# Half of the 64x64 products of a block inverse sent crosswise between the row halves of TensorE

## The chip, the cores and the metric

One core of one Trainium2 chip runs the whole program. The metric is the time of one execution on the device in microseconds (us), the median of the runs shown. Engines are TensorE (PE, its weight loads PEld), VectorE (DVE), ScalarE (ACT), GpSimd (POOL) and SyncE (SP, which here only issues DMAs).

## What is computed

The reference adds three things to x (8 batches, 512 tokens, 256 features): a gated delta rule attention over 32 value heads, a small feed-forward part, and x itself. What this change touches is inside the attention, which works on chunks of 64 tokens. For each chunk it needs the inverse of a unit lower triangular 64x64 matrix, and the reference builds it row by row:

```
attn = -(jnp.einsum('bhcid,bhcjd->bhcij', k_beta, k) * decay_mask)
attn = jnp.where(upper, 0.0, attn)
def _correct_row(a, i):
    row = a[..., i, :]
    corr = jnp.einsum('...j,...jk->...k', row, a)
    corr = corr * (jnp.arange(chunk_size) < i)
    return (a.at[..., i, :].set(row + corr), None)
attn, _ = jax.lax.scan(_correct_row, attn, jnp.arange(1, chunk_size))
attn = attn + jnp.eye(chunk_size, dtype=attn.dtype)
value_corrected = jnp.einsum('bhcij,bhcjd->bhcid', attn, v_beta)
```

After that a state is carried from chunk to chunk (eight chunks), and each chunk's output is normed, gated and projected.

## The kernel before

The eight batches go in four pairs, and for each pair there are 16 key heads with two value heads each: 64 turns of one loop body, called heads here. A pair's two batches lie on the two halves of the 128 partitions: batch 0 on partitions 0 to 63, batch 1 on 64 to 127. A head has 16 units (8 chunks times 2 value heads), each a 64x64 matrix per batch; unit `u` of batch `b` is `tile[half(b), u, :]`.

No scheduler decides the order. Each engine has its own instruction stream, written by the same skeleton: `core` walks the eight chunks of head g, and between its steps it calls `front_piece` for head g + 1, with a step number s from 0 to 23 (three per chunk). So a piece with s = 19 or 20 lies in chunk 6 and one with s = 21 to 23 in chunk 7, and tables of numbers say what runs at which s. Waits between engines are counted semaphores: `after(eng, name, g, n)` waits for the n-th event of that name in head g, `loaded` waits for DMAs.

The inverse of head g + 1 is made so:

- `decayed_squares` (DVE, s = 6) writes the decayed products to `at`. SP sends them through DRAM (`relayout`) so that DVE inverts the 16x16 blocks on the diagonal, all of them at once (`invert_rows`, `join_left`, `join_right`, s = 11 to 15, tile `xi`; `xit` is its transpose).
- `relayout_back` (SP) stores `xi` and `xit` to DRAM and loads the blocks of `xi` back to the diagonal blocks of `dd` with eight DMAs (L325). ACT's own queue loads `xit` the same way to `ee` (s = 17).
- `off_products` (PE, s = 19, L662) multiplies the parts off the diagonal, `off`, with `dd`: 32 products of 64x64, in two groups of eight units. `negated` (ACT, L951) takes each group out of PSUM with a minus sign to `pbd`.
- `fixpoint` (PE, L678) runs three rounds, each of 32 products in two groups: `pbd` times `ee`, then twice `pbd` times `yy`. After each group DVE's `add_round` (L1295, L1299) adds `ee` and writes `yy`, in the last round `bda`. `yy` is the same memory as `at`, and the trace calls it `at`.
- The rounds stand at s = 20, 22 and 23.

A product of unit u and batch b runs with weights and moving data from the 64 rows of b and gives its result on the 64 columns (PSUM partitions) of b:

```
last = mm(ms[n][half(b), v * CH:(v + 1) * CH], pbd[half(b), u, :], src[half(b), u, :],
          start=True, stop=True, tile_position=(b * CH, b * CH))
```

So of the four 64x64 corners of the array only the two on its diagonal are used. `ms[0]` and `ms[1]` are two banks of PSUM, one for each group. `pj[0]` and `pj[1]` are two further banks, the ring through which the projections and transposes of a head go (`fill_ring` on PE, `empty_ring` on ACT). The last four of them, the transposes of v (L610), wait for `silu` 3 of ACT (L929), which waits for DVE's convolution (L1185).

Around this stand, in chunk c: `key_state` (L686), `query_state` (L698), `out_project` (L757), `output_rows` (L748), `solve` (L715, waits for DVE's `residual`, L1305), `update` (L729) and `intra` (L741, waits for ACT's copy L957).

An fp32 product is two instructions of weights and two of data in the trace: 32 products show as x64. One of these is called a pass below.

Of the kernel before, what the change touches and what calls it, by code (L numbers as in the profile page):

```python
# [55 lines left out]
def build(nc, x_in, w_qkvz, w_ba, conv_w, a_log, dt_bias, norm_w, w_out, w_gu, w_proj, consts, out):  # L56
    ctx = ExitStack()
    with ctx:
# [48 lines left out]
        ee = sb("ee", [P, U, CH])  # L107
        pbd = sb("pbd", [P, U, CH])
        st = sb("st", [P, 2, NB, GRP, DH])
        sdec = sb("sdec", [P, NB, GRP, DH])  # L110
# [87 lines left out]
        d_w, d_g, d_ge, d_wo, d_q = sem("d_w"), sem("d_g"), sem("d_ge"), sem("d_wo"), sem("d_q")  # L198
        d_a0, d_a, d_off, d_x0, d_x1, d_dd, d_ee = (sem(n) for n in ("d_a0", "d_a", "d_off", "d_x0", "d_x1", "d_dd", "d_ee"))
        phase = sem("phase")  # L200
# [21 lines left out]

        for name, n in (("proj", RING), ("sskq", 2), ("kk", 2), ("pp", 2), ("yp", 6),
                        ("ks", NC - 1), ("qs", NC - 1), ("wp", NC), ("ds", NC - 1), ("op", NC), ("yt", NC), ("od", NC)):
            counted(name, n)

        for name, n in (("pcopy", RING), ("silu", 4), ("sqs", 2), ("dexp", 1), ("pneg", 2), ("wev", NC), ("wos", 1),
                        ("sso", NC), ("yte", NC), ("ysc", NC)):
            counted(name, n)
# [99 lines left out]
        def _(sp):  # L329
# [102 lines left out]

            def head(g, q, hk, weights=True, stores=True):
# [66 lines left out]
        def _(pe):  # L500
# [149 lines left out]

            def off_products(g, p, n):
                if n == 0:
                    loaded(pe, d_dd, g, GRP * NBLK)
                    loaded(pe, d_off, g, NB * (NBLK - 1))
                    after(pe, "atit", g, 2)
                else:
                    after(pe, "coef", g, 5)
# [8 lines left out]
            def fixpoint(g, p, r, n):  # L666
# [7 lines left out]
                apart(pe)  # L674
                for v in range(8):
                    u = 8 * n + v
                    for b in range(NB):
                        last = mm(ms[n][half(b), v * CH:(v + 1) * CH], pbd[half(b), u, :], src[half(b), u, :],  # L678
                                  start=True, stop=True, tile_position=(b * CH, b * CH))
                last.then_inc(S["yp"], 1)  # L680

# [79 lines left out]
            def front_piece(g, hk, s):  # L761
# [9 lines left out]
                if s == 11:  # L771
                    square_sums(g, 1)
                    chunk_squares(g, p, 1)
                for n in range(2):
                    if s == 19:
                        off_products(g, p, n)
                for n, at_s in enumerate((20, 20, 22, 22, 23, 23)):
                    if s == at_s:
                        fixpoint(g, p, n // 2, n % 2)
                for n in range(RING - 2, RING):  # L780
# [47 lines left out]
        def _(act):  # L828
# [118 lines left out]
            def negated(g, n):  # L947
                after(act, "pp", g, n + 1)
                if n == 0:
                    before(act, "yp", g)  # L950
                fn(pbd[:, 8 * n:8 * n + 8, :], ms[n][:, :].rearrange("p (u c) -> p u c", u=8), ACT.Copy, scale=-1.0  # L951
                   ).then_inc(S["pneg"], 1)
# [24 lines left out]
            def front_piece(g, hk, s):  # L977
# [7 lines left out]
                if s == 16:  # L985
                    output_weights(g, p)
                for n in range(2):
                    if s == 19:
# [55 lines left out]
        def _(dve):  # L1044
# [7 lines left out]

            for t in (xpad, dd, ee, off, xpair):
                dve.memset(t[:], 0.0)
# [235 lines left out]
            def add_round(g, p, r, n):  # L1290
                after(dve, "yp", g, 2 * r + n + 1)
                us = slice(8 * n, 8 * n + 8)
                src = ms[n][:, :].rearrange("p (u c) -> p u c", u=8)
                if r < 2:
                    tt(yy[:, us, :], src, ee[:, us, :], ALU.add).then_inc(S["yadd"], 1)  # L1295
                else:
                    if n == 0:
                        before(dve, "wp", g, 2)
                    tt(bda[:, p, us, :], src, ee[:, us, :], ALU.add).then_inc(S["yadd"], 1)  # L1299

# [192 lines left out]
```

## Time and profile before

| | us |
|---|---|
| median of three runs | 5176.98 |
| lowest, highest | 5168.34, 5177.32 |
| the profiled execution, its time | 5178.37 |
| the same, its span in the trace | 5176.3 |
| TensorE busy | 4793.5 (93%) |
| VectorE busy | 3623.3 (70%) |
| ScalarE busy | 3024.5 (58%) |
| GpSimd busy | 1086.0 (21%) |

The first 560 us or so prepare tokens, the feed-forward part and decay tables; the 64 heads fill the rest, 71.6 us each. The profiled execution lies 1.4 us above the median of the runs. Busy time of TensorE overlaps between instructions, so distances in this document go from the start of one group to the start of the next.

### The profile page before, as it was taken

To read this page: it belongs to the slowest core of one execution; us is meant where nothing else is said; L and a number is where in the kernel's file an instruction comes from. 1 tells how busy PE (TensorE), PEld (TensorE's weight loads), DVE (VectorE), ACT (ScalarE), POOL (GpSimd) and SP (SyncE) were. 2 spreads that over 40 slices of the span, in tenths; PEclk is the share of its full clock that TensorE was granted. 3 is DMA by queue.
4 is the path that set the end of the run, shared out by engine and by line. 5 is a ranking of instruction groups with operands and counts; after the bars stand their busy time and mean duration, and the time that the engine had idled before them with its cause. 6 is when DMAs were issued, how large, how long until landed. Compare 5 with 4: busy or idle time off the path is not lost.

```text
span 5176.3 us, 140889 instructions
## 1 busy us (share of the span) xinstructions
PE 4793.5 (93%) x52272; PEld 3332.8 (64%) x52272; DVE 3623.3 (70%) x6423; ACT 3024.5 (58%) x7909; POOL 1086.0 (21%) x1064
## 2 busy tenths in 40 slices
PE   2777799999999999999999999999999999999998
PEld 1545566666666666666666666666666666666666
DVE  6444477777777677777777767777777777777776
ACT  1222466666666656666666666666666666666665
POOL 0000122222222222222222222222222222222222
PEclk9888899999999999999999999999999999999999
DMA  1111222222222322222222222222222322222221
GB/s 50 31 30 30 82 57 64 53 54 64 57 65 52 79 63 58 64 52 55 64 57 73 68 55 63 58 65 52 57 63 68 77 52 58 61 63 58 64 52 35
DMA packets 686346, 300.56 MB, mean 58 GB/s; under 512 B 599152, under 2 KB 642288, under 8 KB 675440
## 3 DMA queue, kind: packets, MB, share of 16 engines
q1 hardware_dynamic: 546416, 283.18, 21.2%
q10 hardware_dynamic: 139264, 8.42, 1.8%
q8 instruction: 428, 7.01, 0.6%
q14 instruction: 238, 1.95, 0.1%
HBM read 212.76 MB, written 66.07 MB: 54 GB/s over the span
## 4 chain that ended last, share of the span: by engine, by line
issue 51%; PE 26%; POOL 12%; DVE 4%; DMA 3%; ACT 2%; SPq 1%; ACTq 1%; POOLq 0%; DVEq 0%
POOL sdec L1432 5%; PE pj L620 4%; POOL rout L1438 4%; PE dsb L757 3%; PE ms L678 2%; POOL kn L1425 2%; PE pot L570 2%; PE pj L615 2%; PE pj L549 2%; PE ms L549 2%; PE pot L715 2%; PE dsb L729 1%; PE pot L686 1%; POOL gb L1420 1%; PE pod L741 1%
## 5 line engine op out<-in xcount | busy, mean ns | idle before, releaser
L1185 DVE SCALAR_TENSOR_TENSOR cy<-xpad,cw,cy 128x1024 f32<-128x1024 f32 x768 | 1104.9, 1446 | 7.0
L620 PE MATMUL pj<-xnT,wt 128*128 128x512 f32 x2048 | 1013.4, 618 | 27.5 <-DMA xnT<-xnT_d 19.0
L1438 POOL TENSOR_TENSOR rout<-rin,expo 128x2 f32<-128x2 f32 x512 | 358.9, 701 | 2324.3 <-DVE rin L1326 2324.3
L1432 POOL TENSOR_TENSOR sdec<-st,gel 128x512 f32<-128x512 f32 x384 | 402.8, 1049 | 1148.8 <-DVE st L1315 972.0
L757 PE MATMUL dsb<-wo,yT 128*128 128x256 f32 x2048 | 573.4, 402 | 10.5 <-issue 9.4
L620 PEld LDWEIGHTS pj<-xnT,wt 128*128 128x128 f32 x2048 | 349.2, 190 | 354.4 <-issue 340.7
L915 ACT ACTIVATE xpad<-pj 128x512 f32<-128x512 f32 x512 | 304.1, 594 | 361.9 <-PE pj L620 361.9
L615 PE MATMUL pj<-wt,xnT 128*128 128x256 f32 x2048 | 509.9, 392 | 0.0
L974 ACT ACTIVATE yT<-dsb 128x256 f32<-128x256 f32 x512 | 196.6, 384 | 516.6 <-PE dsb L748 516.4
L1315 DVE TENSOR_TENSOR st<-dsb,sdec 128x512 f32<-128x512 f32 x384 | 265.1, 690 | 307.1 <-PE dsb L729 306.7
L907 ACT ACTIVATE arena<-pj 128x512 f32<-128x512 f32 x256 | 152.9, 597 | 471.1 <-issue 323.4
L615 PEld LDWEIGHTS pj<-wt,xnT 128*128 128x128 f32 x2048 | 368.3, 189 | 84.5 <-issue 43.8
L757 PEld LDWEIGHTS dsb<-wo,yT 128*128 128x128 f32 x2048 | 347.7, 189 | 114.4 <-issue 86.3
L729 PEld LDWEIGHTS dsb<-ww,arena 64*128 64x128 f32 x3584 | 235.2, 186 | 272.2 <-issue 268.7
L969 ACT ACTIVATE arena<-arena,rout 128x128 f32<-128x128 f32 x1024 | 350.8, 393 | 30.3 <-POOL rout L1438 30.3
L1305 DVE SCALAR_TENSOR_TENSOR rr<-pot,nge,arena 128x128 f32<-128x128 f32 x896 | 270.3, 343 | 121.3 <-PE pot L686 120.8
L916 ACT ACTIVATE cy<-pj,cw 128x512 f32<-128x512 f32 x512 | 350.0, 684 | 0.0
L715 PE MATMUL pot<-rr,bda 64*64 64x128 f32 x3584 | 293.0, 280 | 54.7 <-DVE rr L1305 34.1
L963 ACT ACTIVATE junk<-arena 128x128 f32<-128x128 f32 x1024 | 315.3, 323 | 37.1 <-DVE arena L1322 28.8
L741 PE MATMUL pod<-ww,arena 64*64 64x128 f32 x4096 | 332.9, 280 | 2.2 <-issue 1.6
L729 PE MATMUL dsb<-ww,arena 64*128 64x128 f32 x3584 | 320.5, 297 | 6.3 <-ACT ww L957 5.9
L904 ACT ACTIVATE arena<-pj,kn 128x256 f32<-128x256 f32 x512 | 200.9, 475 | 156.9 <-PE pj L610 156.9
(163 smaller groups left out, 8427.8 us busy)
## 6 DMA issues: line engine op xcount, KB each, us to landing
qge<-ge_rows SPq DMA_DIRECT2D x64, 1024.0 KB, 6.9
wt<-in_L_attn_W_qkvz SPq DMA_DIRECT2D x64, 768.0 KB, 4.6
gb<-g_rows SPq DMA_DIRECT2D x128, 256.0 KB, 4.1
a_d<-at SPq DMA_DIRECT2D x64, 512.0 KB, 2.7
wo<-in_L_attn_W_out SPq DMA_DIRECT2D x64, 256.0 KB, 2.7
x_d<-xpair SPq DMA_DIRECT2D x128, 128.0 KB, 1.7
ap_<-a_d SPq DMA_DIRECT2D x512, 16.0 KB, 1.8
dd<-x_d SPq DMA_DIRECT2D x512, 16.0 KB, 1.9
```

Source lines behind the costliest of these rows:

```text
L615: last = mm(pj[n % 2][:, v * GRP * DH:(v + 1) * GRP * DH], xnT[:, k, c * P:(c + 1) * P], wt[:, k, 4 * DH:4 * DH + GRP * DH], start=(k == 0 ...
L620: last = mm(pj[n % 2][:, :], wt[:, k, col:col + DH], batch(xnT, k, i), start=(k == 0), stop=(k == KD - 1))
L715: last = mm(pkw[half(b), (GRP + h) * DH:(GRP + h + 1) * DH], bda[half(b), p, c * GRP + h, :], rhs, start=True, stop=True, tile_position=(b ...
L729: last = mm(dsb[:, b, h * DH:(h + 1) * DH], kkd[p][half(b), c * GRP + h, :], ww[half(b), h, :], start=True, stop=True, tile_position=(b * ...
L741: last = mm(po[half(b), h * DH:(h + 1) * DH], it[half(b), p, c * GRP + h, :], ww[half(b), h, :], start=(c == 0), stop=True, skip_group_che ...
L757: last = mm(dsb[:, 0, GRP * DH:GRP * DH + D], yT[:, h, :], wo[:, p, h, :], start=(h == 0), stop=(h == GRP - 1))
L916: last = fn(cy[:, m % 2, i, :], src[:, :], ACT.Copy, scale=cw[:, m, TAPS - 1:TAPS])
L963: last = fn(junk[:, h, :], zz[p][:, j, h, :], ACT.Square, accum_out=ss[:, h:h + 1])
L969: last = fn(zz[p][:, j, h, :], zz[p][:, j, h, :], ACT.Copy, scale=rout[:, h:h + 1])
L1185: stt(y, x[:, :, tap:tap + SEQ], cw[:, kind, tap:tap + 1], y, ALU.mult, ALU.add).then_inc(S["conv"], 1)
L1432: tt(sdec[:, :, :, :], st[:, c % 2, :, :, :], bc(gel[:, p, :, :].rearrange("p h (b c) -> p b h c", b=NB)[:, :, :, c], 3, DH), ALU.mult).th ...
L1438: tt(rout[:, :], rin[:, :], expo[:, 0, 0:GRP], ALU.pow).then_inc(S["routs"], 1)
```

## The change

Units 8 to 15 (the second group) now take the other way through the array: with the data in the rows of one batch and the result on the columns of the other. Unit v (straight) and unit 8 + v (turned) are issued alternately, and a round is one group of 32 products.

- `off_products` issues straight products to `ms[0]` and turned ones to `ms[1]`, so that the negated product of the second group lies on the other batch's partitions. `off_products_back` computes the same eight units again, straight, to `pj[1]` (16 more products), and ACT negates them to a new tile `pback`.
- Rounds 0 and 2 read `pbd` and the moving data of the second group from the rows of the other batch and come home; round 1 goes out from home, with `pback` as weights.
- The addend of round 1 and the moving data of round 0 need `ee` of the second group on the other batch's rows: `eturn`, loaded by eight more DMAs on SP.
- A round's wait covers both groups: both negations, both sums.

```diff
@@ relayout_back (SP), behind blocks_back(sp, 0, dd, d_dd)
+                loaded(sp, d_x1, g, 1)
+                apart(sp)
+                for r in range(GRP * NBLK):
+                    turned = (r + NBLK) % (GRP * NBLK)
+                    sp.dma_start(eturn[turned * BLK:(turned + 1) * BLK, :, (r % NBLK) * BLK:(r % NBLK + 1) * BLK],
+                                 x_d[r * U + U // 2:(r + 1) * U, 1].rearrange("u j i -> j u i")).then_inc(d_et, 16)
@@ off_products (PE)
-                    u = 8 * n + v
+                    cut = slice(v * CH, (v + 1) * CH)
                     for b in range(NB):
-                        last = mm(ms[n][half(b), v * CH:(v + 1) * CH], off[half(b), u, :], dd[half(b), u, :],
-                                  start=True, stop=True, tile_position=(b * CH, b * CH))
+                        straight = tile_product(ms[0][half(b), cut], b, off[half(b), v, :], dd[half(b), v, :], b)
+                        turned = tile_product(ms[1][half(1 - b), cut], 1 - b, off[half(b), 8 + v, :],
+                                              dd[half(b), 8 + v, :], b)
+                straight.then_inc(S["pp"], 1)
+                turned.then_inc(S["pp"], 1)
+
+            def off_products_back(g, p):
+                after(pe, "pcopy", g, RING - 4)
+                apart(pe)
+                for v in range(8):
+                    for b in range(NB):
+                        last = tile_product(pj[1][half(b), v * CH:(v + 1) * CH], b, off[half(b), 8 + v, :],
+                                            dd[half(b), 8 + v, :], b)
                 last.then_inc(S["pp"], 1)
@@ fixpoint (PE)
                 if r == 0:
                     loaded(pe, d_ee, g, GRP * NBLK)
-                    after(pe, "pneg", g, n + 1)
+                    loaded(pe, d_et, g, GRP * NBLK)
+                    after(pe, "pneg", g, 2)
                 else:
-                    after(pe, "yadd", g, 2 * (r - 1) + n + 1)
+                    after(pe, "yadd", g, 2 * r)
+                    if r == 1:
+                        after(pe, "pneg", g, 3)
...
+                        straight = tile_product(ms[0][half(b), cut], b, pbd[half(b), v, :], src[half(b), v, :], b)
+                        if r == 1:
+                            turned = tile_product(ms[1][half(1 - b), cut], 1 - b, pback[half(b), v, :],
+                                                  yy[half(b), 8 + v, :], b)
+                        else:
+                            rhs = yy[half(1 - b), 8 + v, :] if r else eturn[half(1 - b), v, :]
+                            turned = tile_product(ms[1][half(b), cut], b, pbd[half(1 - b), 8 + v, :], rhs, 1 - b)
@@ front_piece (PE)
-                for n, at_s in enumerate((20, 20, 22, 22, 23, 23)):
+                for r, at_s in enumerate((20, 22, 23)):
@@ negated (ACT)
-                for n in range(2):
+                for n in range(3):
                     if s == 19:
                         negated(g, n)
@@ add_round (DVE)
+                add = eturn[:, :, :] if (r, n) == (1, 1) else ee[:, us, :]
```

TensorE in chunks 6 and 7, before (`ms` is the PSUM, `dd`, `off`, `pbd`, `ee` and `at` as above):

```order
L662 MATMUL ms<-dd,off 64x64 [waits atit,d_dd,d_off]
L662 MATMUL ms<-dd,off 64x64 x15
L662 MATMUL ms<-dd,off 64x64 [waits coef]
L662 MATMUL ms<-dd,off 64x64 x15
L729 MATMUL dsb<-ww,arena 128x128 [waits accs,wev,yte]
L729 MATMUL dsb<-ww,arena 128x128 x3
L741 MATMUL pod<-ww,arena 64x128 x4
L678 MATMUL ms<-ee,pbd 64x64 [waits d_ee,pneg]
L678 MATMUL ms<-ee,pbd 64x64 x15
L678 MATMUL ms<-ee,pbd 64x64 [waits d_ee,pneg]
L678 MATMUL ms<-ee,pbd 64x64 x15
```

The same place in the changed kernel (its line numbers are its own), down to the first products of round 0:

```order
L661 MATMUL ms<-dd,off 64x64 x32
L243 REGISTER_ALU
L661 MATMUL pj<-dd,off 64x64 x16
L243 REGISTER_ALU
L759 MATMUL dsb<-ww,arena 128x128 x4
L771 MATMUL pod<-ww,arena 64x128 x4
L243 ISA
L661 MATMUL ms<-ee,pbd 64x64
L661 MATMUL ms<-eturn,pbd 64x64
L661 MATMUL ms<-ee,pbd 64x64
L661 MATMUL ms<-eturn,pbd 64x64
```

Sixteen products have been added behind the first 32, in front of `update` (L729, now L759), and a round alternates between the two groups.

SyncE's queue between the block inverse and the next head's loads, in the changed kernel:

```order
L427 DMA x_d<-xpair 128x256 [waits sub,yadd]
L430 DMA x_d<-xpair 128x256 [waits sub]
L327 DMA dd<-x_d 16x16x16 [waits d_x0]
L327 DMA dd<-x_d 16x16x16 x7
L438 DMA eturn<-x_d 16x8x16 [waits d_x1]
L438 DMA eturn<-x_d 16x8x16 x7
L353 DMA wt<-in_L_attn_W_qkvz 128x2x768 [waits proj]
L358 DMA cw<-in_L_attn_conv_weight 128x4 [waits conv]
```

The eight loads of `eturn` are new there. Before, the next head's weights (`wt`) followed the loads of `dd`.

## Rows read from the trace of the kernel before

**Rows 1.** The page's first part: busy us, share, instructions by engine.

```profile
PE 4793.5 (93%) x52272; PEld 3332.8 (64%) x52272; DVE 3623.3 (70%) x6423; ACT 3024.5 (58%) x7909; POOL 1086.0 (21%) x1064
```

**Rows 2.** Windows, one whole head; columns PE, PEld, DVE, ACT, POOL, clock, DMA share, GB/s.

```profile
2538.82:2610.38 71.56, 69.01 (x793) 48.25 (x789) 52.65 (x93) 44.66 (x119) 16.57 (x16) 1.00 0.25 58
```

**Rows 3.** Timeline of PE, chunks 6 and 7 of one head; columns start, duration.

```profile
2538.82 2.06 PE L662 MATMUL ms<-dd,off 64*64 64x64 f32 x64
2540.81 0.72 PE L729 MATMUL dsb<-ww,arena 64*128 64x128 f32 x8
...
2541.94 2.09 PE L678 MATMUL ms<-ee,pbd 64*64 64x64 f32 x64
2543.96 0.65 PE L686 MATMUL pot<-st,kq 128*64 128x256 f32 x4
...
2546.26 0.65 PE L715 MATMUL pot<-rr,bda 64*64 64x128 f32 x8
2546.75 2.03 PE L678 MATMUL ms<-at,pbd 64*64 64x64 f32 x64
2548.61 0.61 PE L741 MATMUL pod<-ww,arena 64*64 64x128 f32 x8
2549.51 1.09 PE L610 MATMUL pj<-cst,vT 128*128 128x128 f32 x8 [0.29 <-issue]
2550.53 2.08 PE L678 MATMUL ms<-at,pbd 64*64 64x64 f32 x64
2552.55 1.09 PE L610 MATMUL pj<-cst,vT 128*128 128x128 f32 x8
```

**Rows 4.** Timeline of DVE and ACT in the same stretch.

```profile
2540.48 1.06 ACT L951 ACTIVATE pbd<-ms 128x512 f32<-128x512 f32 x2
...
2542.65 1.27 DVE L1185 SCALAR_TENSOR_TENSOR cy<-xpad,cw,cy 128x1024 f32<-128x1024 f32 x1
...
2543.84 1.28 DVE L1295 TENSOR_TENSOR at<-ms,ee 128x512 f32<-128x512 f32 x2
...
2545.04 0.60 DVE L1305 SCALAR_TENSOR_TENSOR rr<-pot,nge,arena 128x128 f32<-128x128 f32 x2
...
2546.49 1.27 DVE L1185 SCALAR_TENSOR_TENSOR cy<-xpad,cw,cy 128x1024 f32<-128x1024 f32 x1
...
2547.83 1.04 ACT L929 ACTIVATE vT<-cy 128x1024 f32<-128x1024 f32 x1
```

**Rows 5.** Timeline of SP's queue in the same stretch, and ee's landing times.

```profile
2533.12 3.76 SPq L325 DMA_DIRECT2D dd<-x_d  x8
2537.06 0.40 SPq L351 DMA_DIRECT2D wt<-in_L_attn_W_qkvz  x1
DMA to landing us min/median/max: 1.6/2.1/5.2
```

**Rows 6.** Timeline of PE: one corner alone, then column halves at 1.2 GHz.

```profile
545.54 1.05 PE L589 MATMUL dsb<-cst,kq 64*64 64x64 f32 x16 [0.74 <-DVE acc L1172]
546.43 0.61 PE L589 MATMUL pot<-cst,kq 64*64 64x64 f32 x8
...
587.99 1.88 PE L633 MATMUL ms<-ones,arena 128*64 128x1 f32 x32
589.72 1.95 PE L647 MATMUL ms<-kq 128*64 128x64 f32 x32
```

**Rows 7.** Windows of PE at that lower clock; columns busy, passes, granted clock, DMA.

```profile
588.00:589.60 1.60, 1.60 (x31) 0.50 0.54 60
```

**Rows 8.** Timeline of PE at the full clock: the same two groups, whole.

```profile
2517.57 1.10 PE L633 MATMUL ms<-ones,arena 128*64 128x1 f32 x32
2518.52 1.13 PE L647 MATMUL ms<-kq 128*64 128x64 f32 x32
```

**Rows 9.** Timeline of PE, windows of 35 and 80 ns behind a pause.

```profile
2517.57 0.22 PE L633 MATMUL ms<-ones,arena 128*64 128x1 f32 x2
2506.53 0.38 PE L729 MATMUL dsb<-ww,arena 64*128 64x128 f32 x2
```

**Rows 10.** Groups of instructions by line: x, busy us, mean ns, idle before.

```profile
L662 PE MATMUL ms<-dd,off 64*64 64x64 f32 x4096 | 134.0, 220 | 22.8 <-DMA dd<-x_d 22.4
L610 PE MATMUL pj<-cst,vT 128*128 128x128 f32 x1024 | 139.9, 280 | 1.4 <-ACT vT L929 1.1 <-issue 0.3
```

More of the change, by code:

```diff
@@ L108, in build @@
         pbd = sb("pbd", [P, U, CH])
+        pback = sb("pback", [P, U // 2, CH])
+        eturn = sb("eturn", [P, U // 2, CH])
         st = sb("st", [P, 2, NB, GRP, DH])
@@ L220, in counted @@
             N[name], S[name] = n, sem(name)
-        for name, n in (("proj", RING), ("sskq", 2), ("kk", 2), ("pp", 2), ("yp", 6),
+        for name, n in (("proj", RING), ("sskq", 2), ("kk", 2), ("pp", 3), ("yp", 6),
                         ("ks", NC - 1), ("qs", NC - 1), ("wp", NC), ("ds", NC - 1), ("op", NC), ("yt", NC), ("od", NC)):
             counted(name, n)
-        for name, n in (("pcopy", RING), ("silu", 4), ("sqs", 2), ("dexp", 1), ("pneg", 2), ("wev", NC), ("wos", 1),
+        for name, n in (("pcopy", RING), ("silu", 4), ("sqs", 2), ("dexp", 1), ("pneg", 3), ("wev", NC), ("wos", 1),
                         ("sso", NC), ("yte", NC), ("ysc", NC)):
@@ L649, in chunk_squares, with tile_product, off_products @@
                 last.then_inc(S["kk"], 1)
[L651 to L657, printed above, removed]
+            def tile_product(out, b, lhsT, rhs, a):
+                return mm(out, lhsT, rhs, start=True, stop=True, tile_position=(a * CH, b * CH))
+            def off_products(g, p):
+                loaded(pe, d_dd, g, GRP * NBLK)
+                loaded(pe, d_off, g, NB * (NBLK - 1))
+                after(pe, "atit", g, 2)
+                after(pe, "coef", g, 5)
@@ L675, in fixpoint @@
                 for v in range(8):
-                    u = 8 * n + v
+                    cut = slice(v * CH, (v + 1) * CH)
                     for b in range(NB):
-                        last = mm(ms[n][half(b), v * CH:(v + 1) * CH], pbd[half(b), u, :], src[half(b), u, :],
-                                  start=True, stop=True, tile_position=(b * CH, b * CH))
-                last.then_inc(S["yp"], 1)
+                        straight = tile_product(ms[0][half(b), cut], b, pbd[half(b), v, :], src[half(b), v, :], b)
[5 more added lines that the diff above has]
+                            turned = tile_product(ms[1][half(b), cut], b, pbd[half(1 - b), 8 + v, :], rhs, 1 - b)
@@ L682, in key_state @@
+                straight.then_inc(S["yp"], 1)
+                turned.then_inc(S["yp"], 1)
             def key_state(g, p, c):
@@ L773, in front_piece @@
                     chunk_squares(g, p, 1)
-                for n in range(2):
-                    if s == 19:
-                        off_products(g, p, n)
-                for n, at_s in enumerate((20, 20, 22, 22, 23, 23)):
+                if s == 19:
+                    off_products(g, p)
+                    off_products_back(g, p)
+                for r, at_s in enumerate((20, 22, 23)):
                     if s == at_s:
-                        fixpoint(g, p, n // 2, n % 2)
+                        fixpoint(g, p, r)
                 for n in range(RING - 2, RING):
@@ L950, in negated @@
                     before(act, "yp", g)
[L951 removed]
+                fn(pbd[:, 8 * n:8 * n + 8, :] if n < 2 else pback[:, :, :],
+                   (ms[0], ms[1], pj[1])[n][:, :].rearrange("p (u c) -> p u c", u=8), ACT.Copy, scale=-1.0
                    ).then_inc(S["pneg"], 1)
@@ L1051, in done_then @@
                 dve.wait_ge(s, n)
-            for t in (xpad, dd, ee, off, xpair):
+            for t in (xpad, dd, ee, eturn, off, xpair):
                 dve.memset(t[:], 0.0)
```

11 lines of the change are left out of this document (5 added, 6 removed).

## The prediction

> **What bounds the kernel now.** I read the busy times first [rows 1]: TensorE 93% of the span, the next engine 70%. Then one head in the windows view [rows 2]: 69.0 of 71.56 us busy at clock 1.00, against 52.7 on DVE and 44.7 on ACT. The whole gap to DVE is 16 us per head, so on average DVE can't take over; it can only in a stretch. The timeline of chunks 6 and 7 [rows 3] shows that TensorE's groups follow each other with no wait but one of 0.29 us. So what TensorE saves is worth its full length until another engine's result is late. The groups by line say the same [rows 10]: over 64 heads the off-diagonal products waited 22.4 us for `dd`, the transposes of v 1.1 us for ACT. I count 64 heads of 71.56 us, and all of the change is inside a head.
>
> **What a pass costs, by corners in use.** The price on which everything hangs is that of a 64-column pass with four corners busy, and no row shows it. What rows show:
> - One corner alone: 16 transposing passes in 546.43 - 545.54 = 0.89 us, 55.6 ns each [rows 6].
> - Two corners on the diagonal: a group of 64 passes takes 1.99 us from start to start [rows 3], 31 ns each with the change of array layout in it. I take 29.2 ns: two column halves need 0.95 us for 32 passes, 29.7 ns, with a little of the same change in it [rows 8].
> - The second corner thus came nearly free. Is a common limit just behind? Passes with only one moving column need 29.7 ns as well [rows 8], so the limit there is not the moving data. It could be the issue of instructions, which would kill the change, or the loading of 64 weight columns. The rows at half clock decide: the same one-column passes take (589.72 - 587.99) / 32 = 54 ns [rows 6] at granted clock 0.50 [rows 7], that is 1.2 GHz, against 29.7 ns at 2.4 GHz. A limit of the queue that feeds the array would not double with the array's clock. So it is the weights, 54 ns for a corner of 64 columns, and the two halves load theirs side by side.
> - Two passes start within a window of 35 ns between column halves [rows 9], and two within 80 ns between row halves, first thing behind a pause. Both kinds of neighbour that four corners need do run at once.
>
> Bounds for a pass with four corners: 14.6 ns (half of 29.2) and 29.2 ns (no gain). I take 14.6 to 15, since both pairings halved fully and nothing seen slows down with the number of streams.
>
> **The change part by part**, per head, times from the start of the off-diagonal products at 2538.82.
> - `off_products`: 64 passes at 14.6 ns are 0.93 us where 1.87 stood. `off_products_back`: 32 more on the diagonal at 29.2, +0.93. Sum **0.0 us**. `update` (L729) starts where it did, at +1.99. The wait for the ring's copy is for one that ACT has long made.
> - Negations: ACT now gets both results at +0.9 and takes 1.06 us for two; before, they ran at +1.66 to +2.72 [rows 4], behind other work of ACT. Round 0 may start at +3.12 as before. The third negation, 0.5 us, pushes ACT's `silu` 2 back; nobody waits for that one soon.
> - The eight loads of `eturn`: SP needs 3.76 us for eight like them [rows 5], and starts them when `dd` is issued, at 2536.88. The last is issued at about 2540.2 and lands 1.9 us or so later (I take `ee`'s 2.1 [rows 5]): +3.4. Each is half as large, so the bounds are +2.8 and +3.5, with a tail to +6.5 by the longest landing of `ee`, 5.2. TensorE is ready at +3.12. So **0 to 0.4 us** of wait before round 0, 0.2 taken. The next head's `wt` is issued 3.5 us later than at 2537.06, and is needed only after 2553: no cost.
> - Round 0: 64 passes, 0.93 us less. It ends at about +4.4 instead of +5.14. Next to be late: DVE's convolution runs from +3.83 to +5.1, the two sums behind it 1.28, the residual 0.6 [rows 4]. These are back to back, with no gap that an earlier round would close: the residual is done at +6.8 as before, and `solve` starts at +6.9 instead of +7.44 [rows 3]. Saved so far 0.5, not 0.93.
> - Round 1: 0.93 less, so `intra` (L741) at about +8.4 instead of +9.79. Saved 1.4. Then the transposes of v wait for `silu` 3: DVE's convolution, at 2546.49 now, can start some 0.4 earlier, behind the residual and one sum, ACT follows at about +8.6 and takes 1.04 [rows 4], so they start at +9.75, not at the +9.1 at which TensorE is there. Before: +10.69. Saved **0.9**; up to 0.9 of two rounds' 1.87 is lost to this chain. Between its ends (nothing lost, or all the time that DVE's order gives, 1.0) I take 0.9, from the row's times.
> - Round 2: 0.93 less, in full: behind it stand only the last transposes, whose copies of 0.8 us each keep pace, and the next head's products. The sums of both groups now come after the round, 1.38 us, with 3 us until `solve` 0 needs them. Saved **1.85** at the end of the chunk.
> - In the next head everything hangs on these times and moves along. The loads of decays (`gb`) wait for `cw`, which waits for the convolution, so they gain only 0.3 us; by the trace they had more slack than that.
>
> Sum: -1.85 us per head, 64 heads: -118 us. The profiled execution's time is 5178.4, so 5060; the median lies 1.4 below it. The ends: with no chain behind it, 3 x 0.93 = 2.8 us or -179; with 0.4 us lost to `eturn` and 17 ns a pass, about -1.2 us or -77. The case's own range is **5005 to 5105**.
>
> **The rivals.**
> 1. *A floor in between.* TensorE starts passes at some fixed least distance f, whatever the corners. All 256 passes before cost 29.2 ns; after, 256 at f and 32 at 29.2. The two are equal at f = 29.2 x 224 / 256 = 25.5 ns. For it: none of the rows averages under 29 ns, whatever it does. Against: two starts within 35 ns [rows 9], and the doubling at half clock. With f near 25.5 the gain is nothing: **5177**, within 10 us.
> 2. *Two at a time* (the slower side). Corners that share rows or columns with both neighbours wait for each other, so that a pass goes on costing 29.2 ns. Then the 32 added passes cost their 0.93 us and nothing is saved: +60 us, **5238**. It decides as soon as the four-corner spacing is above the 25.5 ns just worked out. For it: no row has three corners at work, and the order of issue puts straight and turned products on the same rows one after another. Against: the rows above, each pairing by itself.
> 3. *`eturn` late.* If its last block lands at +5 on most heads instead of +3.4, round 0 starts 1.9 us late, swallows all that it saved and delays `solve` by 1 us: net -0.5 us per head, **5145**. It stands behind `dd` on one queue; only the tail of `ee`'s landings speaks for it.
> 4. *The change doesn't issue what it says.* The written order alternates the two groups in round 0 and 1, and only an interleaving that TensorE undoes would fall under rival 2.
>
> The Trainium skill has a rule against this change: TensorEngine Tiling, Instruction Overhead, says that each matmul has about 60 cycles of overhead, so that one column takes as long as 60, and not to take a tiling factor from a dimension already that small. Read as a limit for the whole engine this is rival 1: 60 cycles at 2.4 GHz are 25 ns, an estimate by its figure, and the sum by it would be within 0.2 us per head of no change. The trace agrees that one column costs as much as 64, but puts it down to each corner by itself.
>
> **How the numbers follow.** Four corners at work 0.72 (its own range 0.66 of that), rival 1 0.10, rival 2 0.12, rival 3 0.06. About 0.2% (10 us) is what a measurement here can tell from no change. Faster: 0.72 + 0.06 + a part of rival 1 = 0.79. Same: 0.07. Slower: 0.14. The range reaches from 5005 over rivals 3 and 1 to 5178 and leaves out rival 2.
>
> **What would show it.** In the trace after: a round of 64 passes 1.0 to 1.1 us from start to start where 2.0 stood; `off_products` and its back part 1.9 together; DVE, not TensorE, as what `solve` of chunk 7 waits for; a new wait of 0.5 to 0.9 us of the transposes of v for ACT; a head of 69.7 us. The prediction is wrong if a round takes 1.6 us or more, if round 0 waits over 1 us for `eturn`, or if the next head loses again what this stretch gained.

## The result, and the profile after

The change is faster by 31 us, not by 117.

| | before | after |
|---|---|---|
| median of the runs | 5177.15 (4 runs, 5168.34 to 5181.35) | 5146.52 (4 runs, 5144.49 to 5156.49) |
| profiled execution, time / span | 5178.37 / 5176.3 | 5156.49 / 5154.4 |
| mean granted clock of TensorE | 0.988 | 0.983 |

The ratio is 0.9947, 95% interval 0.9929 to 0.9965. The time moved the forecast way, by a quarter of the forecast size. It lies outside the case's own range of 5005 to 5105, and inside the range that takes in rivals 1 and 3. The profiled execution after is the slowest of its four, 10 us above the median; that of before is 1.2 us above, so the traces show less of the gain than the medians do.

The page of the changed kernel has these busy times by engine and these two of its DMA queues (packets, MB, share), to be held against [rows 1]:

```profile
PE 4660.3 (90%) x54320; PEld 3175.5 (62%) x54320; DVE 3571.8 (69%) x6424; ACT 3052.9 (59%) x7973; POOL 1087.7 (21%) x1064
...
q1 hardware_dynamic: 620144, 287.40, 22.4%
...
q8 instruction: 444, 7.27, 0.6%
```

TensorE is 133 us less busy and the span only 22 us shorter, so TensorE now stands idle for longer. The timeline of PE in chunks 6 and 7 of one head after (start, duration, [idle before <- releaser]) stands against [rows 3]. Since two tiles alternate there, round 0 shows pass by pass; its first four passes and its last stand here.

```profile
2526.73 1.16 PE L661 MATMUL ms<-dd,off 64*64 64x64 f32 x64
2527.68 1.14 PE L661 MATMUL pj<-dd,off 64*64 64x64 f32 x32
2528.74 0.71 PE L759 MATMUL dsb<-ww,arena 64*128 64x128 f32 x8
2529.39 0.65 PE L771 MATMUL pod<-ww,arena 64*64 64x128 f32 x8
2530.91 0.24 PE L661 MATMUL ms<-ee,pbd 64*64 64x64 f32 x1 [0.86 <-DMA eturn<-x_d]
2530.91 0.27 PE L661 MATMUL ms<-eturn,pbd 64*64 64x64 f32 x1
2530.92 0.27 PE L661 MATMUL ms<-ee,pbd 64*64 64x64 f32 x1
2530.93 0.27 PE L661 MATMUL ms<-eturn,pbd 64*64 64x64 f32 x1
...
2531.85 0.22 PE L661 MATMUL ms<-eturn,pbd 64*64 64x64 f32 x1
2532.00 0.65 PE L716 MATMUL pot<-st,kq 128*64 128x256 f32 x4
...
2536.96 1.09 PE L618 MATMUL pj<-cst,vT 128*128 128x128 f32 x8 [0.64 <-ACT vT L959]
2537.99 1.16 PE L661 MATMUL ms<-at,pbd 64*64 64x64 f32 x64
2539.08 1.09 PE L618 MATMUL pj<-cst,vT 128*128 128x128 f32 x8
```

The products are as cheap as forecast. Off-diagonal products and their back part together take 2528.74 - 2526.73 = 2.01 us, as the two groups did before. Round 0 takes 2531.85 - 2530.91 = 0.94 us for 64 passes, 14.7 ns each, and round 2 is 1.09 us from start to start where 2.02 stood [rows 3]. Two waits are new: 0.86 us for `eturn` and 0.64 us for ACT's `silu` 3.

SP's queue in the same head, and the landing times of the page's DMA part (KB each, median us):

```profile
2520.94 3.77 SPq L327 DMA_DIRECT2D dd<-x_d  x8
2524.83 4.33 SPq L438 DMA_DIRECT2D eturn<-x_d  x8
...
dd<-x_d SPq DMA_DIRECT2D x512, 16.0 KB, 1.9
ee<-x_d ACTq DMA_DIRECT2D x512, 16.0 KB, 2.0
eturn<-x_d SPq DMA_DIRECT2D x512, 8.0 KB, 1.9
```

The eight smaller loads take 4.33 us to issue, not less than `dd`'s 3.77. Over all heads the means are 4.5 us (3.7 to 5.3) and 4.1 (3.8 to 5.1). The last is out at 2529.16 and 1.9 us after that is 2531.06, where round 0 starts (2530.91).

The waits view of PE after (us in total, times, longest), summed over all heads:

```profile
PE pot L745 <- DVE rr L1337: 45.1, 116, 0.6
PE ms L661 <- DMA eturn<-x_d: 39.1, 35, 1.7
PE pj L618 <- ACT vT L959: 33.6, 62, 0.7
PE ms L661 <- DMA dd<-x_d: 30.7, 31, 3.5
...
PE ms L661 <- issue: 17.6, 28, 1.8
```

The same view of before:

```profile
PE pot L715 <- DVE rr L1305: 34.1, 80, 0.7
...
PE ms L662 <- DMA dd<-x_d: 22.4, 29, 4.4
PE ms L678 <- DMA ee<-x_d: 11.6, 25, 1.3
...
PE ms L678 <- issue: 6.1, 10, 1.0
...
PE pj L610 <- ACT vT L929: 1.1, 1, 1.1
```

The last of the five, `issue`, is idle time for which the profile has no releaser. It was in no term of the prediction's sum. The timeline of PE in another head after shows the longest kind:

```profile
2595.63 0.65 PE L745 MATMUL pot<-rr,bda 64*64 64x128 f32 x8
2596.35 1.00 PE L661 MATMUL ms<-dd,off 64*64 64x64 f32 x51
2599.14 0.45 PE L661 MATMUL ms<-dd,off 64*64 64x64 f32 x13 [1.80 <-issue]
2599.41 1.49 PE L661 MATMUL pj<-dd,off 64*64 64x64 f32 x32
2600.83 1.22 PE L759 MATMUL dsb<-ww,arena 64*128 64x128 f32 x8
```

TensorE stops behind the 51st of 64 passes, inside a group that waits for nothing, and resumes 1.80 us later. The windows of PE behind that stop (busy, passes, granted clock, DMA share, GB/s) show what follows:

```profile
2598.00:2600.00 2.00, 0.86 (x33) 1.00 0.13 12
2600.00:2602.00 2.00, 2.00 (x29) 0.51 0.74 189
2602.00:2604.00 2.00, 2.00 (x70) 0.64 0.53 205
```

After about 2 us of rest the granted clock is 0.51, the lower level of 1.2 GHz, and `update` takes 1.22 us instead of 0.71. The same stop, of 1.80 us behind pass 51, stands sixteen heads earlier, in the group that starts at 1450.60: it belongs to a place in the program, not to chance. These two heads take 73.8 and 73.3 us, where the median head takes 70.7, so one such stop costs some 3 us.

I counted the instructions of TensorE's stream, those on registers and semaphores too, from the last branch of the loop to each stop inside a group of the inverse. A stop is counted where two passes of one group start over 0.15 us apart. There are 33 in the trace, and within each pass of the loop all lie at one remainder of 256, give or take one: 161 in the first pass, 28 in the second and third, 52 in the fourth. The instruction queue q8 above moved 444 packets, and the trace has 115657 instructions of TensorE, 260 for each packet. So these are stops at the edges of instruction blocks. The Trainium skill states such a block: Runtime: NRT & Kernel Launch, Instruction fetch mechanics, says that each engine's instruction memory is refilled in 16 KiB blocks of 256 instructions by a DMA queue of its own, and that crossing a boundary is mostly hidden. The block size agrees with the count here. Mostly hidden fits too, as 444 blocks went with 33 such stops; the 1.80 us above are what an edge costs where it isn't hidden.

The trace has the times of q8's packets as well, and they show what ends a stop: 28 of the 33 end 1.2 to 1.5 us after the end of the packet that came last before it, and the other five are stops of 0.2 us each. At the edges of blocks in the heads as a whole the median of this distance is 5.0 us. It is the start of the packet that is late, and not its transfer. For the stop of 1.80 us above, the packet starts at 2596.61, only 0.5 us ahead of the stop, and takes 1.07 us. For all eleven distances of over 1 us it starts 0.5 to 1.1 us ahead and takes 0.97 to 1.42, where the median of all packets takes 1.00.

Counted this way, the stops sum to 8.8 us in 12 before and to 25.5 us in 33 after; 17.8 us of the 25.5 lie in the off-diagonal products and their back part. In the heads (behind 620 us) the granted clock is at its lower level for 15.1 us before and for 54.5 us after. At half the clock those 39 us more cost TensorE 20 us at most, which is an estimate.

### The profile page after: what moved, and what is told of

It is laid out like the page before. It is cut to its first block, busy times and chain, and to the rows that moved or that the text cites. A ratio compares the mean times of both kernels' runs of the same rounds, so it can differ in the third digit from the quotient of the medians.

```text
span 5154.4 us, 145642 instructions
## 1 busy us (share of the span) xinstructions
PE 4660.3 (90%) x54320; PEld 3175.5 (62%) x54320; DVE 3571.8 (69%) x6424; ACT 3052.9 (59%) x7973; POOL 1087.7 (21%) x1064
## 3 DMA queue, kind: packets, MB, share of 16 engines
q1 hardware_dynamic: 620144, 287.40, 22.4%
## 4 chain that ended last, share of the span: by engine, by line
issue 51%; PE 24%; POOL 12%; DVE 5%; DMA 3%; ACT 3%; SPq 2%; ACTq 1%; POOLq 0%; DVEq 0%
POOL sdec L1464 5%; POOL rout L1470 4%; PE pj L628 4%; PE dsb L787 2%; POOL kn L1457 2%; PE pot L578 2%; PE pj L557 2%; PE ms L557 2%; PE pj L623 2%; PE pot L745 1%; PE dsb L759 1%; PE pot L716 1%; PE ms L661 1%; DMA x_d<-xpair 1%; PE ms L641 1%
## 5 line engine op out<-in xcount | busy, mean ns | idle before, releaser
L759 PEld LDWEIGHTS dsb<-ww,arena 64*128 64x128 f32 x3584 | 236.3, 187 | 271.6 <-issue 267.6
L759 PE MATMUL dsb<-ww,arena 64*128 64x128 f32 x3584 | 321.7, 298 | 5.6 <-ACT ww L988 4.1
L716 PE MATMUL pot<-st,kq 128*64 128x256 f32 x1792 | 290.3, 400 | 4.0 <-DVE st L1349 2.2
```

The lines of the kernel that those rows point to most:

```text
L716: last = mm(pkw[half(b), 0:GRP * DH], kq[:, p, c, b, :], st[:, c % 2, b, :, :].rearrange("p h d -> p (h d)"), start=True, stop=True, tile_ ...
L759: last = mm(dsb[:, b, h * DH:(h + 1) * DH], kkd[p][half(b), c * GRP + h, :], ww[half(b), h, :], start=True, stop=True, tile_position=(b * ...
```

## The experiments

To compare whole executions, I worked out from the starts of TensorE's groups when, after a head's first off-diagonal product, certain groups start. The numbers are means over heads 1 to 63 of the profiled execution, in us. The columns "no eturn" to "best" are experiments told below.

| start of | before | after | no `eturn` | silu early | neither | best |
|---|---|---|---|---|---|---|
| round 0 | 3.50 | 4.47 | 3.87 | 4.43 | 3.63 | 3.72 |
| `solve` 7 | 8.00 | 8.18 | 7.99 | 7.97 | 7.59 | 8.10 |
| transposes of v | 10.90 | 10.89 | 10.78 | 10.07 | 9.75 | 10.26 |
| the same behind round 2 | 13.94 | 13.01 | 12.90 | 12.70 | 12.26 | 12.66 |
| next head, mean | 71.63 | 71.25 | 71.08 | 71.21 | 70.60 | 70.97 |
| next head, median | 71.39 | 70.68 | 70.46 | 70.64 | 70.07 | 70.39 |
| stops inside groups, us in all | 8.8 | 25.5 | 36.7 | 32.9 | 49.3 | 38.1 |

### The corners, the loads and the products, each alone

**Four corners undone.** Everything of the change stays, but each product runs on the diagonal, and so round 1 adds `ee` for both groups again:

```
-                        turned = tile_product(ms[1][half(1 - b), cut], 1 - b, off[half(b), 8 + v, :], ...
+                        turned = tile_product(ms[1][half(b), cut], b, off[half(b), 8 + v, :], ...
-                            rhs = yy[half(1 - b), 8 + v, :] if r else eturn[half(1 - b), v, :]
-                            turned = tile_product(ms[1][half(b), cut], b, pbd[half(1 - b), 8 + v, :], rhs, 1 - b)
+                            turned = tile_product(ms[1][half(b), cut], b, pbd[half(b), 8 + v, :], src[half(b), 8 + v, :], b)
```

> The changed kernel with every product straight, on the two diagonal corners; loads, waits, groups and the 16 added products as in the change, same result. Theory A (four corners halve a round, and the rest of the change costs): each of the three rounds and the off-diagonal products cost 0.93 us more on TensorE, minus what the wait for ACT's silu hides (0.7): about +2.5 us per head, some 5300 us. Rival C (the crossing as such does little, the order and the merged waits explain the change's time): under 5180.

Measured 5259.37, ratio 1.016 (1.0143 to 1.0177). That is 41 us under the some 5300 of theory A and far above the 5180 of its rival. So the fourfold use of the array alone is worth 5259 - 5147 = 113 us, 1.8 us per head, although the passes themselves save four times 0.93. One of the four is lost whole: round 0 starts at +4.60 in the mean head of this kernel and at +4.47 in the change, since it waits for `eturn` either way.

**The loads of `eturn` and their wait, on the kernel before.**

```
+                loaded(sp, d_x1, g, 1)
+                apart(sp)
+                for r in range(GRP * NBLK):
+                    turned = (r + NBLK) % (GRP * NBLK)
+                    sp.dma_start(eturn[turned * BLK:(turned + 1) * BLK, :, ...], x_d[...]).then_inc(d_et, 16)
@@ fixpoint, r == 0
+                    loaded(pe, d_et, g, GRP * NBLK)
```

> The kernel before, with the eight loads of eturn added behind those of dd on SP's queue and a wait for them ahead of round 0; nothing reads them. Theory A: the wait puts round 0 about 1.0 us later in a kernel in which TensorE is never idle there, +1.0 us per head, 5230 to 5245 us. Rival B (the loads land in time or the delay is absorbed): within 15 us of 5177.

Measured 5217.8, ratio 1.0077 (1.006 to 1.0094), +41 us, between the two expectations. The forecast had 0 to 0.4 us per head for them, at most 26 us.

**The 16 products and the third negation, on the kernel before.**

```
+                if s == 19:
+                    off_products_back(g, p)
@@ negated (ACT)
-                for n in range(2):
+                for n in range(3):
```

> The kernel before, with the 16 added straight products and the third negation, which nothing reads (round 1 waits for the negation, as in the change). Price by the passes: 32 x 29.2 ns = 0.93 us per head, +60 us, about 5237. If TensorE were not the bound there, or the instruction supply set the pace, it would be under 5200 or over 5260.

Measured 5251.51, ratio 1.0146 (1.0129 to 1.0163), +74 us, 1.16 us per head for 32 passes of 0.93. The stops inside groups are 17.9 us here, 14.8 of them inside the added products, against 8.8 in the kernel before. The two prices, 74 and 41, add to 115. Together, in the kernel with four corners undone, they cost 5259 - 5177 = 82: they overlap by 33 us.

### Does the wait for `eturn` set the time?

**No `eturn`.** The change without the eight loads and the wait:

```
-                loaded(sp, d_x1, g, 1)
...
-                    sp.dma_start(eturn[turned * BLK:(turned + 1) * BLK, :, ...], x_d[...]).then_inc(d_et, 16)
@@ fixpoint, r == 0
-                    loaded(pe, d_et, g, GRP * NBLK)
```

> The changed kernel without the eight loads of eturn and without round 0's wait for them; eturn stays zero, so the second half of the units gets another result. Theory A (the loads are late: round 0 stands at +4.4 us behind the off-diagonal products instead of +3.3, and everything behind moves with it): round 0 goes back to +3.3, solve of chunk 7 then waits for DVE's residual at +6.9 instead of 7.98, a gain of about 0.9 us per head, 5085 to 5105 us against the change's 5147. Rival B (the wait only hides DVE's own lateness): solve stays near +7.9 and the time within 10 us of 5147. If the stalls of about 1.8 us inside the products (no engine waited for) come from the loads' DMA traffic, they go too.

Measured 5137.08 (5132.68 to 5141.22), ratio 0.9921 (0.9904 to 0.9937). This kernel leaves `eturn` at zero. Theory A falls and rival B holds: the time is 9 us from the change's, and `solve` stands at +7.99. The stops did not go with the loads either; they grew. The table says why the gain is small. Round 0 is 0.60 us earlier, `solve` 0.19, the transposes of v 0.11. The waits view of PE in this kernel:

```profile
PE pot L738 <- DVE rr L1330: 55.1, 140, 1.2
PE pj L612 <- ACT vT L952: 39.2, 59, 1.5
...
PE ms L655 <- issue: 18.6, 32, 1.6
PE pj L655 <- issue: 17.4, 7, 2.9
```

Between round 0 and `solve` 0.4 us per head is lost again. Stops inside round 0, 17.2 us in place of 2.4, and the wait for DVE's residual at this `solve`, 10.6 us in place of 4.8, are some 0.3 of it. The wait for `silu` grew from 33.6 to 39.2 us.

**Round 0 straight.** Of the rounds only 1 and 2 use four corners. Round 0 runs in two groups on the diagonal (`first_round`), the second with the negated back part, and `eturn` is first waited for in round 1:

```
+                if s == 20:
+                    first_round(g, p, 0)
+                    first_round(g, p, 1)
+                for r, at_s in ((1, 22), (2, 23)):
```

> The changed kernel with round 0 straight again, in two groups as before (the second group with pback, behind the third negation); rounds 1 and 2 crosswise. The loads of eturn stay, but are waited for in round 1, some 4 us later. Theory A (what round 0's crossing saves is what its wait for eturn takes): no gain is lost, and the waits of round 0 and what follows them go: 5100 to 5145 us. Rival B' (round 0's crossing is a net gain and the loss lies behind it): 5175 or more, as the round costs 0.93 us again.

Measured 5148.39, ratio 0.9948 (0.9935 to 0.9962): 3 us above theory A's range, far below the rival's 5175, and the change's time to within 2 us. So crossing round 0 nets nothing. Its 0.93 us per head pays for waiting until `eturn` is there.

**The loads on GpSimd's queue.** `eturn` no longer stands behind `dd`:

```
-                    sp.dma_start(eturn[...], ...)
@@ front_piece (POOL)
+                if s == 17:
+                    loaded(pool, d_x1, g, 1)
+                        nc.gpsimd.dma_start(eturn[...], ...)
```

> The changed kernel with the eight loads of eturn issued by GpSimd, beside SP's loads of dd and ACT's of ee, instead of behind dd on SP. Theory A: if GpSimd issues one in about 0.5 us they land 3 us earlier and the time is that of the run without the loads, 5130 to 5140. If it needs 1 us or more for each, the last lands no earlier than now: 5147 or more. If the three queues only share what the DMA engines can move, dd and ee land later and the off-diagonal products wait: over 5160.

Measured 5194.31, ratio 1.0039 (1.0026 to 1.0053), worse than before. Five rows of this kernel, two of PE's waits and three landing times of its DMA part:

```profile
PE ms L655 <- DMA dd<-x_d: 61.7, 57, 3.5
...
PE ms L655 <- DMA eturn<-x_d: 19.2, 16, 1.9
...
dd<-x_d SPq DMA_DIRECT2D x512, 16.0 KB, 2.1
ee<-x_d ACTq DMA_DIRECT2D x512, 16.0 KB, 2.3
eturn<-x_d POOLq DMA_DIRECT2D x512, 8.0 KB, 2.5
```

The wait for `eturn` halves, that for `dd` doubles, and a load of `eturn` lands in 2.5 us instead of 1.9. The transfers run at the same time as those of `dd` and `ee`, which land in 2.1 and 2.3 us instead of 1.9 and 2.0. The Trainium skill has this rule, in DMA: Bandwidth & Descriptors, Issuing engines are not separate DMA queues: transfers issued by ScalarE, SyncE or GpSimd run on the same 16 DMA engines and interleave, whichever engine starts them. These rows agree. Stops inside groups are longer here too, 39.5 us.

### Does the wait for `silu` set it?

**Silu early.** The last six convolution steps of DVE stand one to four steps earlier, and `silu` 3 stands at s = 20 in place of 22:

```
-                for n, at_s in enumerate((2, 3, 3, 8, 8, 9, 17, 17, 18, 18, 20, 21)):
+                for n, at_s in enumerate((2, 3, 3, 8, 8, 9, 13, 16, 17, 17, 18, 20)):
@@ front_piece (ACT)
-                if s == 22:
```

> The changed kernel with four of DVE's last convolution steps moved to earlier places where DVE stands idle (steps 13, 16, 17, 20 in place of 17, 18, 20, 21) and ACT's last silu moved from s = 22 to s = 20. Same result. Theory A (between round 1 and the transposes of v the change gives back 0.7 us per head waiting for that silu): the wait goes, about -0.65 us per head, 5100 to 5115 against 5147. If the stalls for the program or the wait for dd take it up again: 5130 or more.

Measured 5150.42 (5143.21 to 5166.75), ratio 0.9941 (0.9927 to 0.9956), no gain over the change. The transposes of v do start 0.82 us earlier in the mean head, but the end of round 2 only 0.31 and the next head 0.04. In this trace PE has no wait for `vT` of any size. Four others have grown or are new:

```profile
PE ms L661 <- DMA eturn<-x_d: 50.3, 43, 1.7
...
PE ms L661 <- issue: 18.3, 35, 1.8
PE dsb L787 <- issue: 15.1, 3, 8.0
...
PE pj L618 <- issue: 13.4, 7, 3.2
```

Stops between two passes of `pbd` times `at` (round 2, above all) went from 6, with 2.2 us, to 29, with 17.6 us. My reading, which no run tests by itself: the wait for `silu` ahead of round 2 had given the next block time to arrive, and without it TensorE reaches the edge before the block does.

**The same moves on the kernel before**, as a control:

> The control: the same two moves in the kernel before. There TensorE reaches the transposes of v later than the silu ends, so theory A expects nothing: within 12 us of 5177. If it gains as much as the other (over 25 us), the wait had nothing to do with the four corners.

Measured 5183.52, ratio 1.0003 (0.9994 to 1.0011): by themselves they change nothing.

**Neither wait.** Both edits, no `eturn` and silu early, in one kernel:

> The change without the eight loads of eturn and without their wait, and with the convolution and silu moved as in the run with silu early. Left out: eturn keeps its zeros, so the second half of the units misses one term of two rounds. Each edit alone was worth little: -10 us without the loads, 0 with silu early, although each took a wait of 0.7 to 1.1 us per head away. Theory waits (the two chains cover for each other, and only with both gone does round 2 end early): some -1.2 us per head against the change, 64 heads, about 5070 to 5090, with the stalls of TensorE no longer than the change's 29 us. Theory supply (TensorE is faster than its instructions arrive, and eats what is freed): 5120 to 5140, stalls inside the groups of the inverse 40 us or more, granted clock at 0.975 or below. If it is 5095 to 5115 both have a share.

Measured 5116.92 (5114.34 to 5118.88), ratio 0.9885 (0.9868 to 0.9901). The edits are worth 9 us and nothing alone, and 30 together, so the two chains did cover for each other. This is 27 us above the upper end of the theory of waits and 3 below the lower end of the theory of supply. The stops are 49.3 us in 62, as the latter wanted, and the clock, 0.977, is a little above its 0.975. Its waits of PE:

```profile
PE pot L738 <- DVE rr L1329: 50.8, 147, 0.6
PE ms L655 <- DMA dd<-x_d: 34.1, 29, 4.4
PE ms L655 <- issue: 30.9, 48, 2.7
```

The time is 2 us above the 5095 to 5115 that was to mean a share for both theories, so I read it as that, with the larger share for supply. With both waits gone, the end of round 2 is 1.68 us earlier than before in the mean head (forecast: 1.85), and the next head starts 1.03 us earlier.

### Are the stops a matter of the instruction stream?

**The stream shifted by 128 instructions.** 128 semaphore increments of TensorE before the first head:

```
+            for _ in range(128):
+                apart(pe)
```

> The changed kernel with 128 more instructions (semaphore increments) in TensorE's stream ahead of the heads, where it waits for tokens anyway: the same instructions in the heads, but every block of 256 instructions ends 128 earlier. Theory D (the stalls inside the products are TensorE waiting for the next block of its program, 256 instructions of 64 bytes): the stalls move to other heads and places, and counted in instructions all lie at one remainder of 256 again, 128 off the present one in the first 16 heads; the time stays within 15 us of 5147, more or less as fewer or more blocks end in the dense stretch. Rival E (they are waits for a semaphore or for data that the profile doesn't name): they stay in the same heads and at the same products.

Measured 5175.04 (5165.23 to 5185.63), ratio 0.9995 (0.9984 to 1.0006), where I expected to stay within 15 us of the change. A row shows what the increments themselves cost, ahead of the first head:

```profile
576.16 5.42 PE L628 MATMUL pj<-xnT,wt 128*128 128x512 f32 x8 [29.23 <-issue]
```

The same group waits 14.71 us in the change, for a DMA. So the first head starts some 14 us later, and the profiled span is 13.5 us longer (5167.9 against 5154.4). The medians differ by 28; the other half I can't place. What the run does tell: in the middle two passes of the loop every stop now lies at remainder 156, where it had been 28, and in the fourth at 180, where it had been 52, and on other heads. 128 more is what the edit adds. In the first pass, where the added instructions are in the count themselves, the remainder is 161 as before. So the stops follow the count of instructions, not the work.

### The best version, and what its loads cost

**Round 0 straight and silu early together:**

> The same two moves on top of the version with round 0 straight, which has neither the wait for eturn nor the wait for the silu. Theory A: 5095 to 5115; the best version if round 0's crossing is worth less than its wait.

Measured 5130.68 (5125.27 to 5137.37), ratio 0.9897 (0.9882 to 0.9911). That is the best complete version, 54 us below the kernel before as measured beside it (5184.67) and, by ratios, 0.5% below the change. It missed its expectation by 16 us, with stops of 38 us.

**The same without the loads of `eturn`:**

> The version with round 0 straight and silu early, without the eight loads of eturn and their wait in round 1. Left out: eturn keeps its zeros, so the second half of the units misses its own term in round 1's sum. In that version nothing waited for eturn, so what goes is the loads themselves: their issue on SP's queue and their share of the DMA engines. Theory traffic (added transfers delay the kernel's other loads and TensorE's instruction blocks): 10 to 30 us below 5131 and the stalls shorter than its 38 us. Theory free (loads that nobody waits for cost nothing): 5125 to 5135, stalls as they were.

Measured 5154.17 (5140.71 to 5168.79), ratio 0.9965 (0.9951 to 0.998). Taking away loads that nobody waited for made the kernel 23 us slower (by the ratios 0.7%, 35 us) and less even: the executions lie within 28 us instead of 12. Neither theory had that. The profiled execution is the fastest of the five, so its trace shows little of the loss. Its stops sum to 34.4 us in 25, fewer and longer than 38.1 in 46. TensorE's stream has the same length as in the best version, and the long stops stand at the same places. Here is one in the best version's timeline of PE:

```profile
2167.50 0.55 PE L661 MATMUL pj<-dd,off 64*64 64x64 f32 x12
2169.39 0.80 PE L661 MATMUL pj<-dd,off 64*64 64x64 f32 x20 [1.34 <-issue]
```

The same place without the loads:

```profile
2167.65 0.55 PE L655 MATMUL pj<-dd,off 64*64 64x64 f32 x12
2170.92 0.80 PE L655 MATMUL pj<-dd,off 64*64 64x64 f32 x20 [2.71 <-issue]
```

So an instruction count sets where TensorE stops, and something else for how long. TensorE's stream is unchanged and there is less traffic of loads, yet the stop is twice as long. The block's own packet takes about as long in both, 1.17 us with the loads and 1.04 without, but it starts at 2166.88 in the one and at 2168.60 in the other. The edit also takes nine instructions per head out of SP's stream. Whether that matters wasn't tried, and the slowdown stays unexplained.

## Why the prediction was right and wrong

The time stands near rival 3's number and outside the forecast's own range. One of the forecast's own signs of being wrong came: the next head loses again more than half of what this stretch gained.

- **The price of a pass, right.** Four corners at 14.6 to 15 ns, measured 14.7. Reading the half-clock rows as a limit of each corner [rows 6, 7] was sound. Rivals 1 and 2 are out: both needed 25.5 ns or more. Rival 4 as well.
- **"Sum 0.0 us" for the products, right in the median head and short in the mean.** `update` starts at +2.02 in the median head, +2.01 before. In the mean head it starts at +2.36, +2.05 before: 0.3 us is lost there to stops and to the slow clock behind them. The sum stood for two changes of 0.93 each way, and the added one costs 1.16 us per head when it is made alone.
- **"The last is issued at about 2540.2 and lands 1.9 us or so later: +3.4", the first step that failed.** The landing was right (1.9), the issue was not: +2.4 after the head's start, not +1.4, since eight half-size loads take 4.33 us of SP's queue. I had costed the queue at 3.3 us, below the row that I quoted, 3.76 us for eight [rows 5]. So "0 to 0.4 us of wait, 0.2 taken" became a start of round 0 that is 1.16 us later in the median head. In the mean head it is 0.97, of which 0.3 was lost ahead of `update`; the waits for `eturn` sum to 39.1 us, 0.6 per head, where those for `ee` were 11.6. Rival 3 had this mechanism and a chance of 0.06. Its time, 5145, is close by coincidence: it let the last block land at +5, and in the trace that lands at +4.1 in the median head (+2.9 to +4.9).
- **"Saved so far 0.5" at `solve`.** Measured -0.18. Without the wait for `eturn` it was 0.01, and 0.41 with neither wait, so what stands between round 0 and `solve` is also tighter than I had it: DVE's `rr` makes TensorE wait 45 to 55 us in all, before 34, and the stops grow there.
- **"Saved 0.9" at the transposes of v.** The wait of 0.64 us for `silu` came as forecast (0.5 to 0.9), but from a start that was later: nothing saved there. Silu early alone brings 0.82. (The forecast's own +8.6 and 1.04 make +9.64, not +9.75, and its ends work out at 4999 and 5101, not 5005 and 5105; nothing hangs on either.)
- **"Round 2: 0.93 less, in full", right.** 13.94 to 13.01 from a row where nothing had been saved.
- **"In the next head everything hangs on these times and moves along", the second step that failed.** Of 0.93 us saved at the end of round 2, 0.38 is left when the next head starts. By the waits of PE 0.23 of the loss is DVE's residual and `dd`: the residual's wait grew by 6.6 us outside this chunk's `solve`, that for `dd` by 30.7 - 22.4 = 8.3, and both together are 14.9 / 64. Another 0.2 is gone by `solve` 0 in the mean head and not in the median one, so it falls on disturbed heads; stops and the lower clock behind them do that, but the share wasn't measured. The last 0.1 has no name. In every version of the table 0.5 to 0.8 us is lost in this stretch.
- **Not in the sum at all: the supply of instructions.** I had asked which engine is late, and never whether TensorE gets its own program. Groups of 64 passes with their weights are 128 instructions. In 0.94 us that is 136 a microsecond, twice the pace before. Stops inside the groups went from 8.8 to 25.5 us, and to 33 to 49 in the versions of the table that took a wait away.

The account in the mean head: 1.85 forecast, less 0.68 at `solve` (0.5 against -0.18), less 0.2 more up to the transposes of v (forecast 0.4 gained there, measured 0.19), less 0.55 behind round 2, leaves 0.4. Measured 0.38, times 64 is 24 us; the spans differ by 22, the medians by 31.

What stays open: what makes the fetch of a block start late. The loads of `eturn` aren't it alone: on the kernel before, they came with a single stop inside the groups, of 0.2 us, and the best version without them had longer stops at the same places. The pace of the passes matters: with four corners undone, which keeps the stream and the loads and slows the passes alone, the stops are 4.8 us instead of 25.5. It isn't all either: the kernel before with 16 added products has slow passes throughout and 17.9 us of stops.

## What to carry to other kernels

Products of 64 rows and 64 columns run four at a time on the array, and here that brought 113 us, against 82 for the added products and loads that it needs. Before counting on it, price the loads that bring operands to the other half by their time on the issuing queue, not by their bytes. Once the passes are so short, look in the trace for idle time with no releaser inside a group, count all of the engine's instructions modulo 256 to it, set it against the packets of the instruction queue, and reckon with part of a removed wait coming back as such stops.

## What I had not expected of the hardware

- Stops of TensorE of up to 1.8 us inside the changed kernel's groups (3.8 in the best version without loads) at edges of 256 instructions, 1.2 to 1.5 us after the end of an instruction packet, and behind a long one a granted clock of 0.51.
- Four passes, one for each corner, that start within 20 ns: 2530.91, 2530.91, 2530.92, 2530.93.
- 8 KB loads (16x8x16) that take SP's queue no less time than 16 KB loads (16x16x16): 4.5 us for eight in the mean head against 4.1.
- 128 semaphore increments of TensorE with no work between them follow each other at 0.15 us, 19 us in all.
